# Sorted experts whose results are scattered back tile by tile, and attention sums made for two steps together

## What is computed

```
xn = layernorm(x)
# attention: 16 heads of 8 numbers, q and k normalised, causal, per sequence of 256 rows
scores = einsum('bhqd,bhkd->bhqk', q, k) * scale
attn   = softmax(scores + causal)
a      = einsum('bhqk,bhkd->bhqd', attn, v) @ W_O.T
# experts: each row goes to the one of 8 experts with the largest gate logit
top    = max(softmax(xn @ gate_w.T));  share = top / (top + 1e-8)
y      = gelu(xn @ w1[expert]) @ w2[expert] * share
f      = layernorm(y) * gamma + beta
x      = x + a + f
```

## Time and profile before

| | us |
|---|---|
| median of 3 runs | 1202.88 |
| lowest and highest | 1201.29, 1203.2 |
| the profiled execution | 1206.21 |
| its span, first to last instruction | 1204.1 |

### The profile page before, as it was taken

How to read it: one execution, slowest core, us unless ns; L and a number is a source line. 1 busy time by engine, 2 the same in 40 slices (tenths; PEclk the granted TensorE clock), 3 DMA queues, 4 the chain that set the end, 5 groups by cost and what they waited for, 6 DMA issues and landing times. The chain is left out here.

```text
span 1204.1 us, 15402 instructions
## 1 busy us (share of the span) xinstructions
PE 620.6 (52%) x4314; PEld 480.7 (40%) x4314; DVE 888.5 (74%) x2129; ACT 399.4 (33%) x807; POOL 392.3 (33%) x404
## 2 busy tenths in 40 slices
PE   5400000000000176579999987306699999467675
PEld 3200000000000065467777765204588888334554
DVE  5898888888888975648667663155769888879485
ACT  2430100000000111455656541123166666254221
POOL 0015555555554422463455400323001111003131
PEclk9955555555555568869999998858789999778886
DMA  2000000000000000023000013110000000100000
GB/s 46 1 0 1 0 0 0 0 0 0 0 0 0 9 1 10 1 56 110 26 7 7 26 36 108 44 24 2 19 14 20 20 20 15 45 0 1 1 18 17
DMA packets 35819, 21.11 MB, mean 18 GB/s; under 512 B 8208, under 2 KB 34400, under 8 KB 35776
## 3 DMA queue, kind: packets, MB, share of 16 engines
q1 hardware_dynamic: 34752, 18.48, 5.6%
q0 software_dynamic: 1024, 2.10, 0.6%
HBM read 15.46 MB, written 5.11 MB: 17 GB/s over the span
## 5 line engine op out<-in xcount | busy, mean ns | idle before, releaser
L737 PE MATMUL l0f_gate<-xnT,l0f_w_gate 128*128 128x512 f32 x8 | 7.4, 1084 | 370.8 <-DMA l0f_w_out<-in_l_w_o 359.9
L737 PEld LDWEIGHTS l0f_gate<-xnT,l0f_w_gate 128*128 128x128 f32 x8 | 2.3, 323 | 374.8 <-DMA l0f_w_out<-in_l_w_o 360.4
L1417 DVE TENSOR_REDUCE l1a_low_top<-l1a_score 128x2 f32<-128x512 f32 (+1 forms) x96 | 66.3, 690 | 65.5 <-PE l1a_score L1297 64.3
L1385 ACT ACTIVATE l1a_weights<-l1a_score,l1a_low_top 128x128 f32<-128x128 f32 (+1 forms) x256 | 89.2, 423 | 38.3 <-DVE l1a_low_top L1417 35.1
L1251 POOL TENSOR_TENSOR l1a_q_of<-l1a_q_rows,l_quad_of 128x1024 fp32r<-128x1024 f32 x32 | 59.9, 1896 | 42.0 <-ACT l1a_q_rows L1374 42.0
L443 POOL TENSOR_TENSOR l0s_to_v<-l0s_exp_b,l_qkv 128x512 f32<-128x512 f32 x31 | 38.3, 1257 | 105.8 <-ACT l0s_exp_b L463 105.8
L2107 DVE SCALAR_TENSOR_TENSOR l2e_mixed<-l2e_down,l2e_scaled,l2e_mixed 128x128 f32<-128x128 f32 x256 | 71.7, 343 | 0.2 <-PE l2e_down L2009 0.2
L2009 PEld LDWEIGHTS l2e_down<-l2e_wd,l2e_hidden 128*128 128x128 f32 x512 | 67.2, 193 | 11.0 <-DVE l2e_hidden L2125 6.2
L2009 PE MATMUL l2e_down<-l2e_wd,l2e_hidden 128*128 128x128 f32 x512 | 69.0, 278 | 3.0 <-DVE l2e_hidden L2125 3.0
L1440 DVE COPY l1a_weightsT<-l1a_flip 128x512 f32<-128x512 f32 x96 | 65.4, 681 | 1.5 <-PE l1a_flip L1330 1.5
L1294 PE MATMUL l1a_score<-l1a_k_rows,l1a_q_of 128*128 128x128 f32 (+1 forms) x256 | 55.2, 320 | 12.1 <-ACT l1a_weights L1385 6.4
(11 more groups left out here) (438 smaller groups left out, 2059.3 us busy)
## 6 DMA issues: line engine op xcount, KB each, us to landing
l1e_w<-in_l_w SPq DMA_DIRECT2D x46, 128.0 KB, 2.1
l2e_wgu<-in_l_wgu SPq DMA_DIRECT2D x16, 128.0 KB, 2.1
l_rows<-l1r_rows SPq DMA_DIRECT2D x1, 1472.0 KB, 6.7
l_done<-l1e_done SPq DMA_DIRECT2D x23, 64.0 KB, 1.6
x_sb<-in_x SPq DMA_DIRECT2D x4, 256.0 KB, 3.7
l2e_wd<-in_l_wd SPq DMA_DIRECT2D x16, 64.0 KB, 1.8
out<-x_sb SPq DMA_DIRECT2D x8, 128.0 KB, 1.8
l3m_w<-in_l_w SPq DMA_DIRECT2D x2, 256.0 KB, 3.2
```

Source lines behind the costliest of these rows:

```text
L1385: last = nc.scalar.activation(weights[s % 2][:, n * width:(n + 1) * width], score[s % 2][:, n * width:(n + 1) * width], ACT.Exp, bias=low_ ...
L1417: nc.vector.tensor_reduce(low_top[:, s % 2, 0:len(heads)], score[s % 2][:, :].rearrange("p (h k) -> p h k", k=key_tiles * P), AX.X, ALU.ma ...
```

## The change

In the attention, the sums of two steps are made together, at odd steps only. `weightsT` has four buffers. ScalarE's first `take` of the sequence before moves from step 1 to step 2. TensorE waits for VectorE's copy of step s - 2 before the transposes of step s.

For the sorting, each normalised row carries a 129th column with its own row number, and each row of the cleared buffer a number beyond the real rows. So a sorted row knows where its result belongs, and an empty one has a place of its own after them. GpSimd's clearing and drawing and SyncE's DMA of the cleared buffer move from the attention to the layer norm before it (`zero` and `issue`); the DMA stands there behind the loads of the layer's small weights.

In the experts, GpSimd scatters each tile's result as soon as VectorE has copied it (`return_rows`), 23 indirect DMAs, and adds beta to x after the last. SyncE stores nothing more; it loads weights after each down projection, of which 10 tiles' are now held instead of 14, and at the end loads the 2048 result rows with four plain DMAs. The 16 multiplications by the share are gone: the share enters through the variance and the factor of the normalisation, by two small products on VectorE. TensorE transposes rows two tiles ahead, into three buffers. The diff, cut to its core:

```diff
@@ class Route
-        self.rows = sb("rows", [P, self.tiles, D])
+        self.sent = [sb(f"sent{i}", [P, NT, columns]) for i in range(choices)]
+        self.xn = self.sent[0][:, :, 0:D]
+        self.rows = sb("rows", [P, self.tiles, columns])
-    def draw(self):
+    def zero(self):
         pool = self.core.nc.gpsimd
         pool.memset(self.rows[:, :, :], 0.0).then_inc(self.blank, 1)
+        pool.wait_ge(self.blank, 1)
+        pool.iota(self.rows[:, :, D:D + 1].bitcast(I32), [[P, self.tiles], [1, 1]], base=N * self.choices,
+                  channel_multiplier=1).then_inc(self.blank, 1)
+        for i in range(self.choices):
+            pool.iota(self.sent[i][:, :, D:D + 1].bitcast(I32), [[P, NT], [1, 1]], base=i * N, channel_multiplier=1)
...
-    def clear_rows(self, sp):
-        sp.wait_ge(self.blank, 1)
+    def issue(self, sp):
+        sp.wait_ge(self.blank, 2)
         sp.dma_start(self.rows_dram.rearrange("(t p) d -> p t d", p=P), self.rows[:, :, :]).then_inc(self.blanked, 16)
...
-                                    self.core.xn[:, t, :], None).then_inc(self.spread, 16)
+                                    self.sent[i][:, t, :], None).then_inc(self.spread, 16)
...
+    def return_rows(self, done, j):
+        self.core.nc.gpsimd.indirect_dma_start(
+            self.done_dram, bass.IndirectOffsetOnAxis(ap=self.rows[:, j, D:D + 1].bitcast(I32), axis=0),
+            done[:, j, :], None).then_inc(self.returned, 16)
+
+    def load_results(self, sp, out, i):
+        sp.wait_ge(self.returned, 16 * self.tiles)
+        for c in range(NC):
+            rows = self.done_dram[i * N + c * CH:i * N + (c + 1) * CH, :]
+            sp.dma_start(out[:, c * TPC:(c + 1) * TPC, :], rows.rearrange("(t p) d -> p t d", p=P)).then_inc(self.loaded, 16)
@@ def l1_attention
-        weightsT = [sb(f"weightsT{i}", [P, CH]) for i in range(2)]
+        weightsT = [sb(f"weightsT{i}", [P, CH]) for i in range(4)]
...
+                        if not (first and s < 2):
+                            pe.wait_ge(moved, b * STEPS + (s - 1))
                         for n in range(4):
                             last = nc.tensor.transpose(flip[s % 2][:, n * P:(n + 1) * P],
...
-                        if s >= 1:
+                        if s % 2:
                             if s == 1 and not first:
+                                sums(b - 1, 1 - i, STEPS - 1)
                                 pe.wait_ge(ctx_taken, b * 2 - 1)
                             if s in (3, 5) and not first:
                                 project(b - 1, (3, 5).index(s))
+                            if s > 1:
+                                sums(b, i, s - 2)
                             sums(b, i, s - 1)
-                        elif not first:
-                            sums(b - 1, 1 - i, STEPS - 1)
...
-                        if s == 1 and not first:
+                        if s == 2 and not first:
                             take(b - 1, 1)
@@ class Experts
-    HELD = 14
+    HELD = 10
@@ def l1_experts
-                for j in range(T):
-                    sp.wait_ge(down_taken, j + 1)
-                    if j + Experts.HELD < T:
-                        experts.load(sp, route, j + Experts.HELD)
-                    sp.dma_start(route.done_dram[j * P:(j + 1) * P, :], done[:, j, :]).then_inc(stored, 16)
+                for j in range(T - HELD):
+                    sp.wait_ge(downed, j + 1)
+                    experts.load(sp, route, j + HELD)
+                route.load_results(sp, mixed, 0)
...
+                for j in range(T):
+                    pool.wait_ge(down_taken, j + 1)
+                    route.return_rows(done, j)
                 pool.wait_ge(affine_in, 32)
                 nc.gpsimd.tensor_tensor(core.x[:, :, :], core.x[:, :, :], rep(beta[:, :], 1, NT), ALU.add).then_inc(shifted_x, 1)
-                pool.wait_ge(stored, 16 * T)
-                for t in range(NT):
-                    nc.gpsimd.indirect_dma_start(mixed[:, t, :], None, route.done_dram,
-                                                 bass.IndirectOffsetOnAxis(ap=route.slot[0][:, t:t + 1], axis=0)).then_inc(returned, 16)
...
                 turn(0)
+                turn(1)
                 climb(0)
                 for j in range(T):
+                    if j + 2 < T:
+                        turn(j + 2)
                     if j + 1 < T:
-                        turn(j + 1)
                         climb(j + 1)
                     descend(j)
...
-                for t in range(NT):
-                    act.wait_ge(returned, 16 * NT)
-                    nc.scalar.activation(mixed[:, t, :], mixed[:, t, :], ACT.Identity, scale=share[:, t:t + 1]).then_inc(weighed, 1)
...
+                nc.vector.tensor_tensor(mean_var[:, :, 1], mean_var[:, :, 1], scale[:, :], ALU.mult).then_inc(var_ready, 1)
                 dve.wait_ge(std_ready, 1)
                 order.then(nc.vector.reciprocal(rstd[:, :], rstd[:, :]))
+                order.then(nc.vector.tensor_tensor(rstd[:, :], rstd[:, :], share[:, :], ALU.mult))
```

More of the change, by code:

```diff
@@ L826, with __init__ @@
 class Route:
-    def __init__(self, core, local, stage, experts, choices, dram):
+    def __init__(self, core, local, stage, experts, choices, columns, drams):
         def sb(n, shape, dtype=F32):
@@ L838, in __init__ @@
         self.hit = [sb(f"hit{i}", [P, NT, experts]) for i in range(choices)]
-        self.any_hit = self.hit[0]
-        self.top, self.best, self.spare = sb("top", [P, NT]), sb("best", [P, NT]), sb("spare", [P, NT, experts])
+        self.any_hit = sb("any_hit", [P, NT, experts]) if choices > 1 else self.hit[0]
+        self.top = [sb(f"top{i}", [P, NT]) for i in range(choices)]
+        self.best, self.spare = sb("best", [P, NT]), sb("spare", [P, NT, experts])
         self.total, self.upto = sb("total", [P, experts, NT]), sb("upto", [P, experts, NT])
@@ L1511, in l1_experts @@
     HALVES = F1 // P
-    T = route.tiles
+    T, HELD = route.tiles, Experts.HELD
     with ExitStack() as local:
@@ L1573, in turn @@
                         pe.wait_ge(turned_taken, j - 1)
-                    nc.tensor.transpose(turned[j % 2][:, 0:P], route.rows[:, j, :], core.eye[:, :]).then_inc(turned_made, 1)
+                    nc.tensor.transpose(turned[j % 2][:, 0:P], route.rows[:, j, 0:D], core.eye[:, :]).then_inc(turned_made, 1)
                 def climb(j):
@@ L1582, in climb @@
                         cols = slice(half * P, (half + 1) * P)
-                        last = nc.tensor.matmul(up[j % 2][:, cols], experts.w1[:, j % Experts.HELD, cols], rowsT[j % 2][:, :],
+                        last = nc.tensor.matmul(up[j % 2][:, cols], experts.w1[:, j % HELD, cols], rowsT[j % 3][:, :],
                                                 start=True, stop=True)
@@ L1591, in descend @@
                     for half in range(HALVES):
-                        last = nc.tensor.matmul(down[j % 2][:, 0:P], hidden[j % 2][:, half, :], experts.w2[:, j % Experts.HELD, half, :],
+                        last = nc.tensor.matmul(down[j % 2][:, 0:P], hidden[j % 2][:, half, :], experts.w2[:, j % HELD, half, :],
                                                 start=half == 0, stop=half == HALVES - 1)
@@ L1634, in take_rows @@
                     dve.wait_ge(turned_made, j + 1)
[L1635 to L1637 removed]
+                    if j >= 3:
+                        dve.wait_ge(upped, j - 2)
+                    nc.vector.tensor_copy(rowsT[j % 3][:, :], turned[j % 2][:, 0:P]).then_inc(turned_taken, 1)
                 take_rows(0)
+                take_rows(1)
                 dve.wait_ge(exped, 1)
@@ L2560, in l3_mixer, with scratch @@
         l3_mlp(core, hT, y, loads[2], four)
-def scratch(nc, stage, tiles):
-    return [nc.dram_tensor(f"{stage}_{n}", (tiles * P, D), F32, kind="Internal").ap() for n in ("rows", "done")]
+def scratch(nc, stage, tiles, choices, columns):
+    return [nc.dram_tensor(f"{stage}_{n}", shape, F32, kind="Internal").ap()
+            for n, shape in (("rows", (tiles * P, columns)), ("done", (choices * N + tiles * P, D)))]
 def build(nc, io, out_dram):
```

80 lines of the change are left out of this document (41 added, 39 removed).

## The result

| | before | after |
|---|---|---|
| time, median of 4 runs | 1202.91 us | 1165.39 us |
| lowest to highest | 1201.29 to 1203.20 | 1165.10 to 1165.60 |
| profiled execution: time, span | 1206.21, 1204.1 | 1165.53, 1163.3 |

The ratio is 0.9691, with a 95% interval of 0.9674 to 0.9707: 37.5 us less. The forecast was 1161, with a range of 1151 to 1179.

A forecast was written before the change was run, and what follows sets the result against it. It took TensorE's gaps at width changes to bound the attention, and TensorE's hole plus a gather tail the experts. 1206.2 - 12 (attention) - 30 (experts) = 1164.2, less 3.3 carried over: 1161 us, range 1151 to 1179.

The forecast's parts named there:

- Attention, -12 forecast: Pairing sums saves 47 of 96 TensorE visits to the 32-wide matmul form, 0.37 us each: 12 us, bounds 5 and 17.
- The two places that give back: Attention: VectorE's end of a batch (0.6 us) and ScalarE's copy of the sums (0.1 us) return 0.7 us a batch.
- Norm and the moves on GpSimd, 0: GpSimd's clearing and fills moved into the layer norm hide behind VectorE's statistics: 0, bounds 0 and 2 us.
- The clearing transfer, 0 to 1 us: The 1.5 MB clearing DMA ahead of the router weights lands in 6.7 us, about when those are issued: 0 to 1 us.
- Start of the experts: GpSimd's beta addition holds VectorE's 16-element operation for 3.41 us; moved behind the scatters, first result in SBUF at about 723.6.
- Low clock for four more tiles: Expert loop: after the first result, four more tiles at the low clock, 1.9 us each, until 731.2.
- Scatters, 1.27 us each: Expert loop: GpSimd's scatters take 0.97 us with 0.30 between; 18 more take 22.9 us, the last issued at 755.0.
- Rivals B: The expert loop doesn't quicken, results every 1.74 us, the last 8.5 us later: 1169 us; chance 0.06.
- C: Scatters beside the expert loop slower than in the attention, 2.5 us each, the last 24.6 later: 1185 us; chance 0.08.
- Weights of 13 tiles: Loading 13 tiles' weights in the expert loop at 1.6 us each, up to 745, is hidden or nearly so.
- Tail: After the last scatter: fetch 1.33 us later, load 5.5 us, rows back 28.6 us earlier; statistics to square root 4.6 us.
- The carry-over of 3.3 us: The plain runs' median lay 3.3 us below the profiled execution; subtracting that again took the sum from 1164.2 to 1161.

The follow-up runs named there:

- the bases: The changed kernel run again unaltered, twice, on other chips beside later variants: 1174.08 us and 1173.03 us (ratios to before 0.9729 and 0.9719).
- e1: From the changed kernel, the pairing undone: TensorE sums each step by itself again, one step behind; 1184.56 us, ratio to before 0.9825.
- e5: From the changed kernel, the 1.5 MB clearing transfer issued at the start of the attention instead of in the norm; 1171.17 us, ratio to before 0.9698.
- c_again: The changed kernel itself, unaltered, run again as base beside e5 and two other variants; 1174.08 us, ratio to before 0.9729.
- e3: From the changed kernel, GpSimd's addition of beta to x put ahead of the scatters again; 1178.49 us, ratio to before 0.9783.
- e2: From the changed kernel, the expert transposes issued one tile ahead instead of two; 1181.93 us, ratio to before 0.9800.
- c_third: The changed kernel itself, unaltered, run once more as base beside e6, e10 and another variant; 1173.03 us, ratio to before 0.9719.
- e6: From the changed kernel, the loads of the last 13 tiles' weights in the expert loop left out; 1174.80 us, ratio to before 0.9737.
- e10: From the changed kernel with late clearing and early square-root table, SP reads the last 13 tiles' expert numbers during the attention; 1168.57 us, ratio to before 0.9687.
- e4: From the changed kernel, results stored by SP and fetched by 16 GpSimd gathers in place of the scatters; 1187.66 us, ratio to before 0.9848.

## Why the prediction was right, point by point

The forecast of 1161 was 4.4 us below 1165.39, and the range held it; it also holds the changed kernel's time on the other chips. Against the working:

- **Attention, -12 forecast, -14.1 in the profile after, -10 to -11 in the bases.** Right in that the visits cost and pairing saves them (e1), and within its bounds; the sum was right partly by luck. It counted 17.4 us of gaps less 5.4 given back, and nothing for the loads of the pairs. Measured, the idle time of the loads falls by only 7.1 us, as the waits for ScalarE grow by 9.4, and the loads themselves get 6.9 shorter, of which 6.35 at the sums. The two places that give back can't be told apart in this wait, since VectorE's work at step 6 reaches TensorE through ScalarE too; at 9.4 us against 0.7 a sequence they were undersized.
- **Norm and the moves on GpSimd, 0.** Right. VectorE's normalisation takes 4.19 us with the odd pitch, as before, and the norm keeps its length.
- **The clearing transfer, 0 to 1 us: mis-sized, it costs 2.0 us of the stage and 2.6 at the router's load** (e5 against c_again, and against the profile after). I took its 6.7 us to landing from the kernel before, issued with rows of 512 bytes; with the odd pitch it takes 11.9, and 11.0 at its old place in e5. It was therefore not nearly over when the router weights were issued 6.7 us behind it. The pitch, which I had weighed only for VectorE, is the likely reason: at the old place nothing else about the transfer differs but 0.8% more bytes.
- **Start of the experts.** First result forecast 4.0 us after the stage's start, in SBUF at 4.3. The removal of the hold is right (e3).
- **Low clock for four more tiles behind the first result: wrong, there was none.** The granted clock is 0.50 at 711 to 713 and 0.82 at 713 to 715, that is full from 713.7; the second result comes 1.2 us after the first and the next 1.0 apart, not 1.9. Without the hold TensorE had hardly paused since the stage's start: its matmuls are busy 3.5 of the first 4.0 us, against 1.7 of the first 4.8 before. GpSimd was the bound from the second scatter on, which I had only as a bound of my range.
- **Scatters, 1.27 us each: exact** in the profile after, and they cost the loop nothing (results 1.0 us apart with and without them). The last ended 33.5 us after the start, forecast 35.4. Rivals B and C didn't occur (e2 shows what B would have been).
- **Weights of 13 tiles.** SP issued them 1.75 us apart (12 intervals in 21.0 us) against an estimate of 1.6, and TensorE did wait for them, 4.2 us in all. Still hidden, but closely: the last result was ready 2.0 us before its scatter began (739.76 + 0.29 to 742.09).
- **Tail.** Landing and fetch 1.28 us (forecast 1.33), load 5.4 (5.5), statistics to the root's table 4.67 (4.6).
- **The carry-over of 3.3 us: the step that made the forecast miss.** It treated the distance between the one profiled execution of before and the median as a constant of the kernel. After, the profiled execution (1165.53) lies 0.14 from the median. Without it the sum stands at 1164.2. That this lies 1.3 us from the profiled 1165.5 is luck in part: attention and experts gained 46.2 us instead of 42, and 5.5 went elsewhere (layer 0 ended 2.2 later, norm and projections took 2.0 more, the rest 1.3).

What the first comparison hid: attention and experts differ between profiles of one and the same kernel. The change is worth 37.5 us there and some 33 in the groups of c_again and c_third, whose profiles show the late starts.

**Open.** Why TensorE reports some products up to 3 us after the end that the profile gives them. It is not the transfer of weights (e6), not SP's register reads (e10), and not the way the variants lie in memory, as the unaltered kernel has it too (c_again). Nor is it the chip alone: the loops of e2 and e4 have none, on the chip where those of e1 and e3 have many. The Trainium skill ("Runtime: NRT & Kernel Launch", Instruction fetch mechanics) says that straight code is streamed with its block crossings mostly hidden. The expert loop is such code, and the profile after agrees: four transfers of instructions lie in its loop and no report is late. In c_again's loop there are four as well, against 24 late starts, so they don't go one for one. Whether the supply of instructions has another part in it no run here tells.

## What to carry to other kernels

Look for an engine that switches between two shapes of matmul, count the visits and not the matmuls, and bundle them until another engine ends the wait; beyond that point (here two steps) all or nearly all of the offer is given back. An indirect transfer per tile beside the loop is free as long as the loop's own period is near GpSimd's 1.27 us (here 1.0), where the same transfers in a block at the end cost all their issue times. When a large transfer is moved, look at what small loads are queued behind it, and take its duration for its new row pitch. Before an engine is called late on a finished product, compare its start with the semaphore update, not with the modelled end of the matmul.

## What the runs showed of the hardware that I had not expected

- Clearing 1.5 MB of DRAM from rows of 516 bytes took 10.6 to 11.9 us in the 13 profiles where rows of 512 bytes took 6.7, while reading the same 516-byte rows back took 7.3 to 7.8, no more than before (7.8). A load of 4 KB behind it took 4.1 to 5.7 us instead of 1.5 or 1.6.
- The same program had 181.5, 184.5 and 185.3 us of attention and 30.2, 36.7 and 36.3 us to its last expert result in three profiled executions, with Gelus and copies that start up to 2.6 us after the end given for TensorE's product in the slower two, and in all three 0.02 us after TensorE's semaphore update, wherever one is recorded.
- 768 weight loads of 32 columns took 28.70 us in groups of a step each, 22.35 with two steps together and 21.74 with four.
- VectorE's operation on 16 elements is held until the very end of a 4.6 us GpSimd operation, while a GpSimd scatter beside a VectorE copy of 0.43 us loses at most 0.20 us, and ends 0.83 to 0.87 us after the copy.
